# Attention in straight-line code, and the output projection's inputs formed one half ahead

## The reference

```python
x = x + gated_linear_attention(layernorm(x))
y = layernorm(x)
h = y + softmax_attention(rmsnorm(y, ln1_w)) @ wo.T   # 16 heads of 16
logits = rmsnorm(h, ln2_w) @ gate_w.T                 # 8 experts, the best 2 and their softmax
x = x + h + sum over the two experts of share * (silu(t @ w1.T) * (t @ w3.T)) @ w2.T
```

## Time and profile before

| | us |
|---|---|
| median of 3 runs | 3438.69 (3434.74 to 3439.25) |
| profiled execution | 3437.48 |
| its span in the trace | 3435.9 |
| stage a | 0 to 787 |
| stage b, softmax attention | 787 to 2223.4 |
| stage c, output projection and router | 2223.4 to 2465.6 |
| stage r | 2465.6 to 2590 |
| stage d, experts | 2590 to 3342.6 |
| stage e, combination | 3342.6 to 3435.9 |

### The profile page before, as it was taken

One profiled execution on the slowest core, in us unless ns is written; L12 is line 12 of the kernel. 1 busy time (PEld: TensorE's weight loads), 2 busy tenths in 40 slices (PEclk: granted clock), 3 DMA queues, 4 the chain that ended last, 5 costly groups with the idle time before them and its releaser, 6 DMA issues. The chain is left out here.

```text
span 3435.9 us, 64564 instructions
## 1 busy us (share of the span) xinstructions
PE 2978.2 (87%) x18668; PEld 1894.2 (55%) x18669; DVE 2315.4 (67%) x3776; ACT 1836.9 (53%) x3407; POOL 613.2 (18%) x974
## 2 busy tenths in 40 slices
PE   5888888876999999999999999666577999999970
PEld 4666666653444444444444444255466888888860
DVE  5677777646888888888888888244594444444436
ACT  3555555530888888888888888622142333333320
POOL 1212222210000000000000000000133444444430
PEclk7999999975999999999999999977688999999995
DMA  1332232322222222222222222177431111111129
GB/s 35 111 110 99 98 102 100 108 99 83 63 66 64 64 64 63 65 64 63 63 63 63 63 63 63 35 235 238 132 116 37 50 49 49 50 49 50 49 62 367
DMA packets 194561, 297.57 MB, mean 87 GB/s; under 512 B 31656, under 2 KB 117952, under 8 KB 194512
## 3 DMA queue, kind: packets, MB, share of 16 engines
q1 hardware_dynamic: 148688, 218.81, 20.3%
q0 software_dynamic: 18176, 52.45, 4.6%
q10 hardware_dynamic: 27648, 25.69, 2.5%
HBM read 167.28 MB, written 127.40 MB: 86 GB/s over the span
## 5 line engine op out<-in xcount | busy, mean ns | idle before, releaser
L816 DVE TENSOR_REDUCE b_mxq<-b_p_m 128x1 f32<-128x1024 f32 x1024 | 1205.9, 1219 | 159.9 <-PE b_p_m L838 159.8
L755 ACT ACTIVATE b_probs<-b_p_e 128x512 f32<-128x512 f32 x2048 | 1065.9, 605 | 283.5 <-PE b_p_e L877 277.2
L877 PE MATMUL b_p_e<-b_qst,b_kst 64*128 64x512 f32 x2048 | 643.9, 472 | 6.7 <-ACT b_probs L755 6.7
L838 PE MATMUL b_p_m<-b_kst,b_qst 64*128 64x512 f32 x2048 | 608.4, 423 | 28.6 <-DMA b_vst<-v_d 23.6
L852 PE MATMUL b_p_o<-b_probs,b_vst 128*32 128x512 f32 x4104 | 546.6, 605 | 0.7 <-ACT b_probs L755 0.7
L877 PEld LDWEIGHTS b_p_e<-b_qst,b_kst 64*128 64x128 f32 x2048 | 251.2, 184 | 507.5 <-ACT b_probs L755 416.3
L838 PEld LDWEIGHTS b_p_m<-b_kst,b_qst 64*128 64x128 f32 x2048 | 341.9, 189 | 180.6 <-DVE b_mxq L816 130.0
L1456 ACT ACTIVATE d_act<-d_p_up 128x512 f32<-128x512 f32 x136 | 81.2, 597 | 494.4 <-PE d_p_up L1518 494.4
L787 POOL DMA_DIRECT2D o_d<-b_oT x64 | 36.2, 566 | 1292.8 <-ACT b_oT L745 1292.8
L1533 PE MATMUL d_p_y<-w2T,d_hT 128*128 x1096 | 258.7, 379 | 0.8 <-ACT d_hT L1450 0.8
L1518 PE MATMUL d_p_up<-up_hi,d_xh 128*128 x544 | 250.2, 460 | 5.3 <-DVE d_xl L1475 1.5
(11 more groups left out here) (254 smaller groups left out, 4071.9 us busy)
## 6 DMA issues: line engine op xcount, KB each, us to landing
b_qst<-qk_d SPq DMA_DIRECT2D x384, 64.0 KB
b_kst<-qk_d SPq DMA_DIRECT2D x384, 64.0 KB
x1y_d<-a_x1y SPq DMA_DIRECT2D x32, 512.0 KB, 4.1
qk_d<-a_hi SPq DMA_DIRECT2D x32, 512.0 KB, 2.8
qk_d<-a_lo SPq DMA_DIRECT2D x32, 512.0 KB, 3.7
v_d<-a_v_s SPq DMA_DIRECT2D x16, 1024.0 KB, 6.9
b_vst<-v_d SPq DMA_DIRECT2D x64, 256.0 KB
o_d<-b_oT POOLq DMA_DIRECT2D x64, 256.0 KB, 2.6
```

The costliest lines, as they stand in the source:

```text
L755: nc.scalar.activation(probs[e // 2 % 4][:, (e % 2) * 512:(e % 2 + 1) * 512], p_e[(slot(e) if more1 else e) % EB][:], ACT.Exp, scale=SCALE ...
L816: V_.reduce_max(mxq[half][:, h, qt:qt + 1], p_m[j % 2][:], AX.X).then_inc(s["m_red"], 1)
L838: mm(p_m[j % 2][:, kh * 512:(kh + 1) * 512], qst[r][rows(h), qt * P:(qt + 1) * P], kst[r][rows(h), kh * 512:(kh + 1) * 512], start=True, s ...
L877: mm(p_e[u % EB][:], kst[r][rows(h), kt * P:(kt + 1) * P], qst[r][rows(h), a * 512:(a + 1) * 512], start=True, stop=True).then_inc(s["e_ps ...
```

## The change

In stage b every engine's program is laid out for all 64 pairs without a loop; the waits compare with constants. Behind its last pair SyncE waits until 56 pairs are stored, loads the sums of the first seven batches (14 loads) into one tile `den`, VectorE takes one reciprocal of 128 x 896, and SyncE stores the inverses to `rd_d` and waits for that store.

In stage c the loop over batches is gone too. The inverses of batches 0 to 6 are in memory when it begins; only those of batch 7 are formed there, once, in `sums`. SyncE's first loads are c_oin, c_rd and c_xy of half 0, then the weights, then c_oin and c_rd of half 1, then the sums. In its body it loads c_oin and c_rd two halves ahead, as soon as c_oT(n) is formed. VectorE forms c_oT(n+1) as the first thing of body(n), before c_h(n).

```diff
-def softmax_attention(nc, ctx, qk_d, v_d, o_d, n_batches=8):
+def softmax_attention(nc, ctx, qk_d, v_d, o_d, rd_d, n_batches=8):
...
+    BEFORE = 2 * (n_batches - 1)
+    den = sb("den", [P, BEFORE, 64])
...
+    o_sums = o_d.rearrange("b g (h a e) q -> b a (g h) e q", h=2, a=2)
...
     def pairs(eng, body):
-        with eng.Fori(0, STEPS - 1) as i:
-            for r in range(RING):
-                body(i * RING + r, i, r, True, True, True)
-        for r in range(RING):
-            body((STEPS - 1) * RING + r, STEPS - 1, r, r < RING - 1, r < RING - 2, r < RING - 3)
+        for pair in range(PAIRS):
+            body(pair, pair // RING, pair % RING, pair < PAIRS - 1, pair < PAIRS - 2, pair < PAIRS - 3)
...
         pairs(sp, body)
+        sp.wait_ge(s["o_stored"], 16 * (PAIRS - 8))
+        for n in range(BEFORE):
+            sp.dma_start(den[:, n], o_sums[n // 2, n % 2, :, 16, :].rearrange("g (c j) -> g c j", c=8)).then_inc(s["den_in"], 16)
+        sp.wait_ge(s["den_done"], 1)
+        sp.dma_start(rd_d[0:n_batches - 1].rearrange("b a g (c j) -> (g c) (b a) j", c=8), den[:]).then_inc(s["den_out"], 16)
+        sp.wait_ge(s["den_out"], 16)
...
         pairs(dve, body)
+        dve.wait_ge(s["den_in"], 16 * BEFORE)
+        V_.reciprocal(den[:], den[:]).then_inc(s["den_done"], 1)
...
+    N = 2 * n_batches
     def halves(eng, body):
-        body(0, 0, 0, 0, False, True, n_batches > 1)
-        body(1, 1, 0, 1, True, n_batches > 1, n_batches > 1)
-        if n_batches > 2:
-            with eng.Fori(1, n_batches - 1) as b:
-                body(b * 2, 0, b, b, True, True, True)
-                body(b * 2 + 1, 1, b, b + 1, True, True, True)
...
+        for n in range(N):
+            body(n, n % 2, n // 2, (n + 1) // 2, n > 0, n + 1 < N)
...
-            sp.wait_ge(s[f"rec_st{half}"], b * 16 + 16)
+            if b == n_batches - 1:
+                sp.wait_ge(s["sums_out"], 16)
...
-        def body(n, half, b, b_next, before, after, after2):
-            if after2:
-                sp.wait_ge(s["recip_done"], n + 1)
-                load_sums(half, b + 1)
-            if after:
-                if before:
-                    sp.wait_ge(s["oT_done"], n)
-                load_output(1 - half, b_next)
-                load_inverses(1 - half, b_next)
+        def body(n, half, b, b_next, before, after):
+            if n + 2 < N:
+                sp.wait_ge(s["oT_done"], n + 1)
+                load_output(half, b + 1)
+                load_inverses(half, b + 1)
...
+        act.wait_ge(s["sums_done"], 1)
+        act.dma_start(rd_d[n_batches - 1].rearrange("a g (c j) -> (g c) a j", c=8), sums[:]).then_inc(s["sums_out"], 16)
...
         def normalised(n, half, b, before):
...
-            if before:
+            if n > 1:
                 dve.wait_ge(s["h_ps"], n - 1)
...
-        for half in (0, 1):
-            inverses(half, half, 0)
+        normalised(0, 0, 0, False)
         dve.wait_ge(s["wT_ps"], 1)
...
-        normalised(0, 0, 0, False)
+        dve.wait_ge(s["sums_in"], 32)
+        V_.reciprocal(sums[:], sums[:]).then_inc(s["sums_done"], 1)
...
-            if after2:
-                inverses(n + 2, half, b + 1)
+            if after:
+                normalised(n + 1, 1 - half, b_next, before)
             dve.wait_ge(s[f"in{half}"], b * 16 + 16)
...
             if before:
                 choose(n - 1)
-            if after:
-                normalised(n + 1, 1 - half, b_next, before)
```

More of the change, by code:

```diff
@@ L656, in softmax_attention @@
     p_o = ctx.enter_context(nc.psum_tensor("b_p_o", [P, 512], f32))
-    names = ("q_zero", "k_zero", "ident0", "id", *(f"rows{r}" for r in range(RING)), "m_ps", "m_red", "hi_done", "hl_done", "mT_ps", "turn",
-             "e_ps", "e_done", "pv_done", "oT_done", "o_stored", "o_free",
+    names = ("q_zero", "k_zero", "ident0", "id", *(f"rows{r}" for r in range(RING)), "m_ps", "m_red", "hi_done", "hl_done", "mT_ps",
+             "e_ps", "e_done", "pv_done", "oT_done", "o_stored", "o_free", "den_in", "den_done", "den_out",
              *(f"q_in{r}" for r in range(RING)), *(f"m_in{r}" for r in range(RING)), "start")
@@ L774, in split @@
             pool.wait_ge(s["m_red"], pair * 16 + 18)
-            if not isinstance(pair, int) or pair > 0:
+            if pair > 0:
                 pool.wait_ge(s["mT_ps"], pair)
-            pool.sem_inc(s["turn"], 1)
             g.tensor_copy(hl[:, :, 0], mxq[half][:]).then_inc(s["hi_done"], 1)
@@ L917, in output_projection_and_gate @@
     ident, mhalf = sb("ident", [P, P]), sb("mhalf", [P, T])
-    den_in, rec = [sb(f"den_in{r}", [P, 64]) for r in range(2)], [sb(f"rec{r}", [P, 64]) for r in range(2)]
+    sums = sb("sums", [P, 2, 64])
     oin, rd = [sb(f"oin{r}", [P, 2, HT]) for r in range(2)], [sb(f"rd{r}", [P, 2, HT]) for r in range(2)]
@@ L1030, in store, with body @@
             act.dma_start(xg_v[n], xg[half][:]).then_inc(s[f"st{half}"], 16)
-        for half in (0, 1):
-            store_inverses(half, half, 0)
+        act.wait_ge(s["sums_done"], 1)
+        act.dma_start(rd_d[n_batches - 1].rearrange("a g (c j) -> (g c) a j", c=8), sums[:]).then_inc(s["sums_out"], 16)
         act.wait_ge(s["w_in"], 48)
-        def body(n, half, b, b_next, before, after, after2):
+        def body(n, half, b, b_next, before, after):
             n1 = n + 1
-            if after2:
-                store_inverses(n + 2, half, b + 1)
             if before:
@@ L1059, in _ @@
             dve.sem_inc(s[n], c)
-        def inverses(n, half, b):
-            if not isinstance(b, int) or b > 0:
-                dve.wait_ge(s[f"rec_st{half}"], b * 16)
-            dve.wait_ge(s[f"den{half}"], b * 16 + 16)
-            V_.reciprocal(rec[half][:], den_in[half][:]).then_inc(s["recip_done"], 1)
         def normalised(n, half, b, before):
@@ L1638, in layer_kernel @@
         with Stage(nc) as stage:
-            softmax_attention(nc, stage, qk_d, v_d, o_d, B)
+            softmax_attention(nc, stage, qk_d, v_d, o_d, rd_d, B)
         with Stage(nc) as stage:
```

33 lines of the change are left out of this document (9 added, 24 removed).

## The result

The changed kernel takes 3385.8 us (median of 4 runs, 3384.3 to 3387.2) against 3438.4 before: ratio 0.985, 95% interval 0.983 to 0.987. Its profiled execution took 3384.3 us with a span of 3382.6, so 53.3 us less than the span before. The median lies 9 us above the forecast of 3377, inside the stated range and just outside its likely part of 3369 to 3384.

| stretch | before | after | difference | forecast |
|---|---|---|---|---|
| up to the scalar negation of pair 0 (832.3, 830.0) | 832.3 | 830.0 | -2.3 | 0 |
| from there to stage c | 1391.1 | 1386.7 | -4.4 | -4.8 |
| stage c to its first projection matmul | 15.6 | 17.6 | +1.9 | -3 |
| first to last projection | 201.6 | 161.3 | -40.3 | -53.7 |
| last projection to stage r | 25.0 | 24.0 | -1.0 | 0 |

The account below looks back on a forecast made before the run. TensorE's order of work bounds attention; a TensorE, ScalarE, TensorE, VectorE, TensorE chain bounds the projection. Gains 4.8 + 0 + 3 + 53.7 = 61.5 us off 3437.5 give 3376.0, forecast 3377 against the median; range 3354 to 3398, likely 3369 to 3384.

Parts of the forecast that it names:

- Attention unrolled: Attention: each of 60 looped pairs gets 0.08 us shorter as straight code, 4.8 us gained, bounds 0 and 8.
- Rival 5: Attention: straight code runs dry as each pair's new code must arrive first, +100 us, giving 3482 us; chance 0.03.
- Moved sums hidden: Attention's end: loads, reciprocal and store of seven batches' inverses hide before the next stage; cost 0, bounds 0 and 11 us.
- Start: Projection's start: c_oT no longer last, weights queued behind 2 MB are; gain 3 us, bounds 0 and 4.2.
- First half: Projection's first half: its projection and c_h fill 7.8 of its 10.53 us, so 2.7 us gained.
- The other halves: Projection: c_oT one half ahead closes a 3.55 us gap; 14 halves go from 13.64 to 10.0 us, 51.0 gained.
- the low-clock chain of TensorE: Projection: from projection start through router to the next projection, a half takes 10.65 us at the present clock.
- The transfers' term: Projection: DMA work per half, 10.0 us without small packets, over combine's share of 1.05, gives 9.5 us; range 8.1 to 10.5.
- one of its signs of being wrong: Projection: VectorE waits on c_oin, c_rd or c_xy appearing with a cycle above 11 us would show the forecast wrong.
- Stages r, d, e: Stages after the projection: instructions and order unchanged, so a change of 0 was forecast.
- The rivals' clock: Projection's TensorE clock: without 3.5 us idle stretches its fall loses its reason; a mix of halves at both clocks expected.
- rival 1: Projection: TensorE's clock stays low, cycle 10.65 us, 52.4 us less in all, giving 3386 us; chance 0.20.

Follow-up runs that it names:

- run 1: Kernel after, with c_oT of the next half formed after the router's choice again, as in the kernel before: 3425.1 us, ratio 0.997.
- Run 8: Kernel after, with the projection's three weight loads issued first, ahead of the 2 MB for half 0: 3389.0 us, ratio 0.986.
- 3: Kernel after, with the attention's loop put back: 3391.9 us, ratio 0.987.
- 6: Kernel after, with one more 256 KB load of attention output per half, into a tile nothing reads: 3407.2 us, ratio 0.992.
- run 10: Kernel after, with the residual load of half n+1 issued ahead of c_oin and c_rd of half n+2, same queue: 3379.7 us, ratio 0.983.
- run 9: Kernel after, with inverses loaded once (32 KB a half) and spread over partitions by two TensorE matmuls, weights loaded first: 3405.0 us, ratio 0.991.
- run 2: Kernel before, with only c_oT formed one half ahead; its loop and per-half loads of sums stay: 3414.9 us, ratio 0.995.
- Run 7: Kernel after, with one of two 256 KB loads of inverses per half left out, engines' work unchanged, output wrong: 3366.9 us, ratio 0.980.
- Run 11: Kernel after, with the residual of half n+2 issued on ScalarE's queue after its squares of half n: 3388.0 us, ratio 0.985.

## Why the prediction came near, and where it was wrong

- **Attention unrolled**: 4.8 us forecast, 4.5 measured, and again 4.5 and 4.6 in the runs with the loop put back or taken out alone. Over all traces the 63 intervals take 1344.8 to 1345.7 us with the loop (four kernels) and 1340.2 to 1340.8 without it (nine), run 1 excepted, which has 1342.7 for no reason that we know. The step is right: one pair of straight code beside a looped pair gave the price. Rival 5 is out.
- **Moved sums hidden**: right, with far more room than the 3.5 us worked out. The loads issue in 8.96 us, not 15.6: the median of 1.12 came from a queue crowded by other loads and is 0.64 here. The reciprocal takes 5.75, not 7.7, and the store is through in 2.7, not 8: 18 ns a piece on its engine, not 54.
- **Start**: wrong in sign, +1.9 for -3. The landing of the weights behind 2 MB was put 10 us after the stage's start and is at 15.0. Run 8 shows that the queueing is the cause, and that undoing it brings nothing in the end, which the sum had missed: it added the start to the halves as if they were independent. (Runs 1, 3, 6 and 10, which begin the stage with the same loads, have their first projection at 15.7 to 17.3 us, so the 17.6 is the late end of a spread; none has the gain of 3.)
- **First half**: 7.68 us, forecast 7.8. Right.
- **The other halves**: the mechanism is right (run 1 gives it all back) and the cycle is mis-sized, 10.97 for 10.0. Of the two terms, the low-clock chain of TensorE, 10.65, stood up where the clock is low: run 9 shows it bare. The transfers' term was 9.5 and is the one that failed. 3.15 MB in 10.97 us are 287 GB/s, not the 331 behind 9.5: the step took a share of 1.05 from the combine stage for the whole half, while this stage has it for 68 of 125 us only and 0.87 on average. The busy part itself came out at 0.87 x 10.97 = 9.5 us, for 10.0 forecast. The upper bound given, 10.5, was too low as well. The share above 0.9 that the prediction expected did not come, and one of its signs of being wrong did: VectorE waits for c_xy, with full intervals of 11.26, above its 11. The 0.6 us allowed for the small packets isn't shown by itself; the 0.7 of run 2 holds more than them.
- **Stages r, d, e**: -7.2 us with no instruction changed. "All else keeps its instructions" was true and not enough. Without this gain, and the 2.3 us that came before the attention (that mark lies anywhere from 826 to 836 us in the fourteen traces, so it is no gain of the change), the profiled execution would have been 3394, above the likely part of the range. The near hit is part luck: 18 us too much in stage c, 10 got elsewhere.
- **The rivals' clock**: the granted clock rose from 0.75 to 0.81 in the regular halves, a mix of both levels as forecast, but not by the reason forecast, that without a pause of 3.5 us the fall has no cause. In run 9 TensorE's longest pause is 1.36 us, and the granted clock goes from 1.00 through 0.79 to 0.50 between 2305 and 2307 us, with TensorE busy since 2302.00. What sets it isn't shown. What rival 1 takes from the Trainium skill ("TensorE: Matmul & The Clock Gate", HAM oscillation — how this bites in real kernels) is told there of waits longer than the bursts between them, so "wherever DMA is the bound" went beyond it: here TensorE's waits for c_h are 1.5 us on average. Rival 1 would give 3386, which is the time measured, but not for its reason: it needs TensorE without gaps, and TensorE waits 16.3 us for c_h in 125. Run 7, with intervals far below 10.65 on the same TensorE work, excludes it as the bound.

**Open.** Why 256 KB cost 1.3 to 1.6 us when their share of the mean rate is 0.9 (0.262 MB at 287 GB/s), and why the share stays at 0.87 (0.81 with more loads, same order). Bursts with gaps between them are not the answer, as no microsecond in 125 has a share under 0.45. What fits is that the loads of c_oin and c_rd keep only half of the engines busy. While they alone are on their way the share is 0.53, half of the 1.05 that it has with the residual beside them, and each of them has 8 rows outermost where the residual has 128 partitions. A 2 KB packet takes 98 ns, so 128 of them on 8 engines would take 1.57 us and not the 0.78 that the expectations of 6 and 7 reckoned with 16: an estimate, against 1.52 and 1.58 measured over full intervals. With the 9.5 us of work spread evenly at 1.05 the cycle would be some 9.1 us, also an estimate. No run splits these loads in another way, so it stays an argument; that is the experiment to make next. It isn't settled either that the order of run 10 is a gain outside the spread.

## What to carry to other kernels

When a step that waited is moved ahead, price the next bound from the same stretch of the trace with the gap closed, and take the share that this mix of transfers has reached there; a share reached by another stage is a bound, not an estimate. Look at that share microsecond by microsecond: a level of half the full one says more than the mean. Before changing an order of issue, check how long before its use a transfer is issued; at 17 us ahead the order is not what is late. Two terms that hang on one resource don't add: a transfer-bound stage gives an earlier start back, and the small transfers here cost 0.04 us a half as long as something else was the bound. Before crediting a code change in one stage, look at the stages that it did not touch; a loop there can get cheaper or dearer by where its code comes to lie.

## What the runs showed of the hardware

- At the head of stage d's loop TensorE's weight load waits 0.52, 0.32 or 0.26 us for the same instructions, by what lies ahead of them in the program: 6 to 8 us in 32 turns. The Trainium skill ("Runtime: NRT & Kernel Launch", Instruction fetch mechanics) has a taken branch fetch its target by DMA when it lies outside the current window of code. The trace agrees that the place matters, but between 2700 and 3250 us neither the kernel before nor after has a packet on an instruction queue, so a fetch each turn is not what is seen.
- With 64 semaphore increments ahead of them on TensorE (run 5) the weights' transposes start 19.5 us after the stage's start in place of 8.7: 0.17 us each, if the weights landed as before. The stage is only 6.8 us longer, as c_oT had been later than the transposes.
- In stage c of the kernel after the DMA engines' share stands mostly at two levels, 0.95 and above in 68 of 125 us and 0.45 to 0.62 in 35; with c_oin and c_rd alone on their way it is 0.53.
- A reciprocal of 896 columns takes 5.75 us, 6.4 ns a column; one of 64 takes 0.55.
- Issuing four 256 KB loads takes SyncE 2.5 us when the queue is empty (2216.70 to 2219.20) and 8.5 us in the halves: behind a full queue the issue waits, and so does what stands behind it.
- The Trainium skill ("DMA: Bandwidth & Descriptors", Issuing engines are not separate DMA queues) says that a second issuing engine saves issue time only. Run 11 agrees: 10.92 us an interval for 10.95.
